# A fused cross-attention kernel: another order of VectorE's and GpSimd's instructions within a step

## The chip, the cores and the metric

One core of one Trainium2 chip runs the whole kernel. The metric is the device time in microseconds (us) of one execution. An engine here is TensorE (PE in the profile, its weight loads PEld), VectorE (DVE), ScalarE (ACT), GpSimd (POOL) or SyncE (SP), which issues the transfers. Each engine works through its own list of instructions in order, and waits at semaphores for the others and, where it reads what it has just written, for itself.

## The reference

With x of shape (4, 2048, 512) and ctx of shape (4, 77, 384), all float32:

```python
text_p = x @ W_text + b_text                       # 512 -> 512
audio_p = ctx @ W_audio + b_audio                  # 384 -> 512
Q = layer_norm(text_p, g1, beta1)
K = layer_norm(audio_p, g2, beta2)
alpha = softmax(Q @ K.T / sqrt(512))               # 77 keys
out = layer_norm((alpha @ audio_p) @ W_out + b_out + x, g_out, beta_out)
```

The layer norms divide by the root of the variance over 512 features plus 1e-5. All three need a row statistic that is ready only after a product.

## The kernel before, in words

The prologue (about 55 us) folds the small matrices together: the scores of a row of x are one product with a matrix `proj` of its batch (77 score columns, a mean column and the 512 columns of a quadratic form whose dot product with x is the variance of the projected row), and values times `W_out` are one matrix per batch. What is left runs in 32 steps of 256 rows. A step takes the rows as two halves, t = 0 and t = 1, of 128 rows each; below `x_lo`(0) is `x_lo` of the first half. Steps go over the four batches in turn. The engines work at several steps at once: `lag` in the code is how many steps behind the newest one an instruction works.

For a half, in order of the data:

- SP loads 128 rows of x into `xs`, as soon as `hid` of the same half four steps back has been made.
- TensorE transposes them into the one bank `psT` (L1253). ScalarE copies that to `x_hi` (L619), VectorE makes the rest `x_lo` (L854). TensorE's next transposes wait for that `x_lo`, since they write `psT` again.
- TensorE multiplies `x_hi` and `x_lo` with `proj` into two banks (L1322, L1326, then L1333). VectorE adds a constant to the first bank's scores, `sc_part` (L946), adds the second bank's to that, `xs<-psY,sc_part` (L954; the scores lie beside the rows of x), and takes the quadratic sum (L956).
- Once per step VectorE clamps the statistics, `stat_eps` (L968); GpSimd raises them to the power -1/2, `rstd` (L470), and makes `shift2` from it (L474; its tile is `shift` in the rows).
- VectorE makes the `logits` of both halves (L985), then their maximum `neg_max` (L988). ScalarE takes the exponentials into `psD` (L670) and rounds them into `parts` (L678); VectorE makes the rest of `parts` (L997, L998) and `inv_sum`, the reciprocal of the sums (L993).
- TensorE transposes `parts` into `psE` (L1303, L1304), between L1326 and L1333 of the second half; ScalarE copies that to `parts_t` (L684); TensorE multiplies it with the values into the one bank `psO` (L1345).
- VectorE makes `hid` from `psO`, `inv_sum` and `xs` (L976). ScalarE squares it for the variance (L650) and normalises it into `zs` (L661). GpSimd multiplies `zs` by `gain` (L458) and adds `shift` (L464). SP stores a step's 256 rows when both halves' sums are made (L354).

What sets the order of every engine is written out by hand: one function `body` per engine with calls in a fixed order, repeated for each step, and a tail for the last two steps in which calls are written one by one. ScalarE's order in a step is `x_hi`(0), square(0), normalise(0), exponentials, rounding, `x_hi`(1), `parts_t`, square(1), normalise(1). TensorE's is transposes(0), values product(0), `proj` product(0), values product(1), transposes(1), `proj` product(1) with the turned `parts` in between. In the tail GpSimd makes the powers one by one (L487); VectorE's `last_logits` (L1081) wait for them.

Of the kernel before, what the change touches and what calls it, by code (L numbers as in the profile page):

```python
# [33 lines left out]
def cross_attention(nc, x, ctx, w_text, b_text, w_audio, b_audio, w_out, b_out,  # L34
                    g1, beta1, g2, beta2, g_out, beta_out, out):
    B, L, D = x.shape
# [27 lines left out]
    with ExitStack() as stack:  # L64
# [183 lines left out]
        LAST = STEPS - 1  # L248
# [137 lines left out]
        def _(pool):  # L386
# [67 lines left out]
            def gain_of(b, i, t, lag):  # L454

                q = (b - lag) % B
                wait_if_positive(pool, z_ready, T, i, T * (b - lag) + t + 1)
                nc.gpsimd.tensor_tensor(zs[:, q, t, :], zs[:, q, t, :], gain[:], ALU.mult).then_inc(zg_ready, 1)  # L458

            def shift_of(b, i, t, lag):  # L460

                q = (b - lag) % B
                wait_if_positive(pool, zg_ready, T, i, T * (b - lag) + t + 1)
                nc.gpsimd.tensor_tensor(zs[:, q, t, :], zs[:, q, t, :], shift[:], ALU.add).then_inc(out_ready, 1)  # L464

            def body(b, i, live):

                if live(2) or live(4):
                    wait_if_positive(pool, stat_ready, 1, i, b - 1)
                    nc.gpsimd.tensor_tensor(rstd[:, b, :], stat_eps[:, b, :], neg_half[:], ALU.pow).then_inc(rstd_ready, 1)  # L470
                if live(4):
                    q = (b - 4) % B
                    wait_if_positive(pool, rstd_ready, 1, i, b - 1)
                    nc.gpsimd.tensor_tensor(shift2[:, q, :], sc[:, q, :, NX], rstd[:, b, T:2 * T], ALU.mult).then_inc(shift2_ready, 1)  # L474
                if live(5):
                    gain_of(b, i, 1, 5)
                    shift_of(b, i, 1, 5)
                if live(4):
                    gain_of(b, i, 0, 4)
                    shift_of(b, i, 0, 4)  # L480

            written_out(body)


# [4 lines left out]
            def mean_shift(n, j):  # L489
                pool.wait_ge(rstd_ready, n)  # L490
                nc.gpsimd.tensor_tensor(shift2[:, j % B, :], sc[:, j % B, :, NX], rstd[:, j % B, T:2 * T], ALU.mult).then_inc(shift2_ready, 1)

            def late_gain(j, t):
                pool.wait_ge(z_ready, T * j + t + 1)
                nc.gpsimd.tensor_tensor(zs[:, j % B, t, :], zs[:, j % B, t, :], gain[:], ALU.mult).then_inc(zg_ready, 1)

            def late_shift(j, t):
                pool.wait_ge(zg_ready, T * j + t + 1)
                nc.gpsimd.tensor_tensor(zs[:, j % B, t, :], zs[:, j % B, t, :], shift[:], ALU.add).then_inc(out_ready, 1)

            inverse_root(STEPS - 1, (LAST + 1) % B, 0, 2 * T)
            mean_shift(STEPS - 1, LAST - 3)
            late_gain(LAST - 4, 1)
            late_shift(LAST - 4, 1)
            inverse_root(STEPS, (LAST + 2) % B, 0, 1)
            late_gain(LAST - 3, 0)
# [264 lines left out]
        def _(dve):  # L771
# [207 lines left out]
            def shifted_logits(b, i):  # L979
                q = (b - 2) % B  # L980
                wait_if_positive(dve, rstd_ready, 1, i, b - 1)
                wait_if_positive(dve, sc_ready, T, i, T * (b - 2) + T)
                wait_if_positive(dve, prob_ready, T, i, T * (b - 4) + T)
                for t in range(T):
                    nc.vector.scalar_tensor_tensor(logits[:, b % 2, t, :], sc[:, q, t, 1:1 + S], rstd[:, b, t:t + 1],  # L985
                                                   score_d[:, q, :], ALU.mult, ALU.add).then_inc(logits_ready, 1)
                wait_if_positive(dve, logits_ready, T, i, T * (b - 2) + T)
                nc.vector.reduce_max(neg_max[:, q, :], logits[:, b % 2, :, :], axis=AX_X, negate=True).then_inc(max_ready, 1)  # L988

# [11 lines left out]
            def body(b, i, live):  # L1001
                if live(2):
                    scores_and_quad(b - 1, i, 1)
                if live(2) or live(4):
                    guard(b, i, live)
                if live(3):
                    residual(b, i, 0)
                if live(0):
                    lo_part(b, i, 0)
                if live(2):  # L1010
                    shifted_logits(b, i)
                if live(1):
                    part_of_scores(b, i, 0)
                    scores_and_quad(b, i, 0)
                if live(2):
                    prob_rest(b, i)
                if live(3):
                    residual(b, i, 1)
                if live(0):
                    lo_part(b, i, 1)  # L1020
                if live(2):
                    inverse_sum(b, i)
                if live(1):
                    part_of_scores(b, i, 1)


            written_out(body)
# [2 lines left out]
            END = STEPS // B  # L1030
# [63 lines left out]
            residual(0, END, 0)  # L1094
            shifted_logits(0, END)
            part_of_scores(0, END, 0)
            scores_and_quad(0, END, 0)
            prob_rest(0, END)
            score_guard(0, 1, T * LAST + 1)
# [332 lines left out]
```

## Time and profile before

| what | value |
|---|---|
| median of 3 runs | 271.93 us (271.63 to 275.46) |
| profiled execution | 271.35 us, its span 269.6 us |
| TensorE's granted clock, mean of the span | 0.993 |
| TensorE busy | 257.3 us (95%) |
| VectorE busy | 238.0 us (88%) |
| ScalarE busy | 202.1 us (75%) |
| GpSimd busy | 209.3 us (78%) |

Busy time counts the stretches in which an instruction ran, overlaps once. The span is the profiled stretch from the first to the last instruction; the execution's own time has 1.75 us more around it. A start-to-start distance between two neighbours on one engine says more than their durations, since an instruction may begin before the one ahead of it has ended.

### The profile page before, as it was taken

To read this page: it belongs to the slowest core of one execution; us is meant where nothing else is said; L and a number is where in the kernel's file an instruction comes from. 1 tells how busy PE (TensorE), PEld (TensorE's weight loads), DVE (VectorE), ACT (ScalarE), POOL (GpSimd) and SP (SyncE) were. 2 spreads that over 40 slices of the span, in tenths; PEclk is the share of its full clock that TensorE was granted. 3 is DMA by queue.
4 is the path that set the end of the run, shared out by engine and by line. 5 is a ranking of instruction groups with operands and counts; after the bars stand their busy time and mean duration, and the time that the engine had idled before them with its cause. 6 is when DMAs were issued, how large, how long until landed. Compare 5 with 4: busy or idle time off the path is not lost.

```text
span 269.6 us, 5946 instructions
## 1 busy us (share of the span) xinstructions
PE 257.3 (95%) x1667; PEld 232.3 (86%) x1667; DVE 238.0 (88%) x719; ACT 202.1 (75%) x516; POOL 209.3 (78%) x232
## 2 busy tenths in 40 slices
PE   7899999999999999999999999999999999999970
PEld 6678868899999999999999999989999999999830
DVE  3858479879999999999999999899999999999894
ACT  3775267246788888888888888888888888888981
POOL 6075630011599999999999999999999999999985
PEclk9999999999999999999999999999999999999997
DMA  6905199332225445444454444544444444444217
GB/s 203 317 30 186 42 340 347 108 126 91 79 77 189 163 175 172 165 160 163 158 163 169 168 163 153 161 156 156 157 157 157 156 156 156 156 158 168 94 49 272
DMA packets 19456, 43.25 MB, mean 160 GB/s; under 512 B 2050, under 2 KB 2382, under 8 KB 19434
## 3 DMA queue, kind: packets, MB, share of 16 engines
q1 hardware_dynamic: 18810, 41.96, 46.0%
q10 hardware_dynamic: 624, 1.06, 1.2%
q14 instruction: 16, 0.13, 0.2%
q8 instruction: 6, 0.10, 0.1%
HBM read 21.19 MB, written 16.78 MB: 141 GB/s over the span
## 4 chain that ended last, share of the span: by engine, by line
DVE 63%; PE 14%; issue 10%; POOL 5%; ACT 2%; DMA 2%; SPq 1%; DVEq 0%; POOLq 0%; ACTq 0%
DVE x_lo L854 13%; DVE hid L976 13%; DVE waste_dve L956 12%; DVE xs L954 5%; DVE logits L985 5%; DVE neg_max L988 3%; DVE sc_part L946 3%; DMA zs<-in_ctx_dram 2%; DVE parts L998 2%; PE psY L1145 2%; PE psT L1220 1%; DVE stat L956 1%; PE psY L1220 1%; PE psT L1170 1%; POOL zs L464 1%
## 5 line engine op out<-in xcount | busy, mean ns | idle before, releaser
L1322 PE MATMUL psY<-proj,x_hi 128*128 128x336 f32 x512 | 92.4, 322 | 0.0
L1322 PEld LDWEIGHTS psY<-proj,x_hi 128*128 128x128 f32 x512 | 80.8, 188 | 2.8
L464 POOL TENSOR_TENSOR zs<-zs,shift 128x512 f32<-128x512 f32 x55 | 71.0, 1291 | 4.3
L458 POOL TENSOR_TENSOR zs<-zs,gain 128x512 f32<-128x512 f32 x55 | 70.9, 1289 | 1.0 <-ACT zs L661 1.0
L470 POOL TENSOR_TENSOR rstd<-stat_eps,neg_half 128x4 f32<-128x4 f32 x30 | 30.5, 1017 | 32.2 <-DVE stat_eps L968 32.2
L1333 PE MATMUL psY<-proj,x_lo 128*128 128x336 f32 (+1 forms) x256 | 50.5, 319 | 0.0
L956 DVE CUSTOM_DVE_ANT_0 waste_dve<-psY,xs,sums 128x515 bf16<-128x515 f32 x64 | 48.4, 757 | 2.2
L650 ACT ACTIVATE waste_act<-hid,xs 128x512 bf16<-128x512 f32 x60 | 43.0, 717 | 8.6 <-DVE hid L976 8.6
L661 ACT ACTIVATE zs<-hid,shift,rstd 128x512 f32<-128x512 f32 x59 | 47.5, 805 | 0.0
L976 DVE SCALAR_TENSOR_TENSOR hid<-psO,inv_sum,xs 128x512 f32<-128x512 f32 x60 | 44.8, 746 | 0.1
L854 DVE TENSOR_TENSOR x_lo<-psT,x_hi 128x512 fp32r<-128x512 f32 x64 | 43.5, 680 | 0.7 <-ACT x_hi L619 0.5
L619 ACT ACTIVATE x_hi<-psT 128x512 fp32r<-128x512 f32 x64 | 37.6, 588 | 5.7 <-PE psT L1253 5.7
L1253 PE MATMUL psT<-ident,xs 128*128 128x128 f32 x256 | 40.1, 279 | 0.4
L1333 PEld LDWEIGHTS psY<-proj,x_lo 128*128 128x128 f32 x256 | 39.0, 189 | 0.0
L1253 PEld LDWEIGHTS psT<-ident,xs 128*128 128x128 f32 x256 | 29.5, 140 | 10.6 <-DVE x_lo L854 5.0
L684 ACT ACTIVATE parts_t<-psE 128x512 fp32r<-128x512 f32 x31 | 18.6, 599 | 22.5 <-PE psE L1304 22.5
L1345 PE MATMUL psO<-wo_hi,parts_t 128*128 128x512 f32 x60 | 26.7, 445 | 0.1
L1345 PE MATMUL psO<-wo_lo,parts_t 103*128 103x512 f32 x60 | 23.7, 394 | 0.0
L1326 PEld LDWEIGHTS psY<-proj,x_lo 128*128 128x128 f32 x128 | 22.1, 188 | 0.0
L954 DVE TENSOR_TENSOR xs<-psY,sc_part 128x79 f32<-128x79 f32 x64 | 15.4, 240 | 7.5 <-PE psY L1333 0.7
L1326 PE MATMUL psY<-proj,x_lo 128*128 128x256 f32 (+1 forms) x128 | 21.7, 251 | 0.0
L670 ACT ACTIVATE psD<-logits,neg_max 128x77 f32<-128x77 f32 x62 | 19.1, 309 | 2.3 <-DVE neg_max L988 2.3
(264 smaller groups left out, 418.3 us busy)
## 6 DMA issues: line engine op xcount, KB each, us to landing
xs<-in_x_dram SPq DMA_DIRECT2D x64, 256.0 KB, 3.0
out_dram<-zs SPq DMA_DIRECT2D x29, 512.0 KB, 3.9
proj<-proj SPq DMA_DIRECT2D x4, 768.0 KB, 8.5
out_dram<-zs SPq DMA_DIRECT2D x6, 256.0 KB, 2.1
xs<-in_L_xattn_W_text_dram SPq DMA_DIRECT2D x4, 256.0 KB, 3.6
xs<-in_L_xattn_W_out_dram SPq DMA_DIRECT2D x2, 512.0 KB, 4.3
wa<-in_L_xattn_W_audio_dram SPq DMA_DIRECT2D x1, 768.0 KB, 6.3
zs<-in_ctx_dram SPq DMA_DIRECT2D x1, 462.0 KB
```

What stands on the lines that cost most here:

```text
L458: nc.gpsimd.tensor_tensor(zs[:, q, t, :], zs[:, q, t, :], gain[:], ALU.mult).then_inc(zg_ready, 1)
L464: nc.gpsimd.tensor_tensor(zs[:, q, t, :], zs[:, q, t, :], shift[:], ALU.add).then_inc(out_ready, 1)
L650: nc.scalar.activation(waste_act[:, t, :], hid[:, (b - 3) % 2, t, :], ACT.Square, bias=sc[:, q, t, NX:NX + 1], accum_out=stat[:, (b + 1) % ...
L661: nc.scalar.activation(zs[:, q, t, :], hid[:, b % 2, t, :], ACT.Identity, bias=shift2[:, q, t:t + 1], scale=rstd[:, b, T + t:T + t + 1]).t ...
L854: nc.vector.tensor_tensor(x_lo[:, b % 2, t, :], psT[:], f32(x_hi[:, b % 2, t, :]), ALU.subtract).then_inc(x_lo_ready, 1)
L956: nc.vector.tensor_tensor_reduce(out=waste_dve[:, t, 0:QUAD_W], in0=psY[:, t, QUAD_AT:QUAD_AT + QUAD_W], in1=xs_rows[:, q, t, X_AT - 1:X_A ...
L976: nc.vector.scalar_tensor_tensor(hid[:, (b - 3) % 2, t, :], psO[:], inv_sum[:, q, t:t + 1], xs[:, q, t, :], ALU.mult, ALU.add).then_inc(hi ...
L1253: last = nc.tensor.transpose(psT[:, k * P:(k + 1) * P], xs[:, b, t, k * P:(k + 1) * P], ident[:])
L1322: nc.tensor.matmul(psY[:, t, to:to + HALF], x_hi[:, par, t, k * P:(k + 1) * P], proj[:, q, k, right * HALF:(right + 1) * HALF], start=(k = ...
L1326: last = nc.tensor.matmul(psY[:, t, B_AT + SW + k * P:512], x_lo[:, par, t, k * P:(k + 1) * P], proj[:, q, k, SW + k * P:HALF], start=Fals ...
L1333: last = nc.tensor.matmul(psY[:, t, 512 + skip:512 + HALF], x_lo[:, par, t, k * P:(k + 1) * P], proj[:, q, k, HALF + skip:ROW_W], start=Fa ...
L1345: last = nc.tensor.matmul(psO[:], parts_t[0:rows, (b - lag) % 2, t, n, :], v[0:rows, q, :], start=(n == 0), stop=(n == 1))
```

## The change

TensorE's, ScalarE's and SP's lists stay as they are. VectorE's `sc_part` of the second half moves from behind the reciprocal to in front of `x_lo` of the second half; the maximum becomes a call of its own, `largest`, and stands behind `sc_part` of the first half; the reciprocal moves ahead of the rest of `parts`. GpSimd makes both products and then both sums of one step, all five steps behind, where it had made the second half five behind and the first half four behind, each product followed by its sum. The tails of both engines are adapted.

```diff
                 if live(5):
+                    gain_of(b, i, 0, 5)
                     gain_of(b, i, 1, 5)
+                    shift_of(b, i, 0, 5)
                     shift_of(b, i, 1, 5)
-                if live(4):
-                    gain_of(b, i, 0, 4)
-                    shift_of(b, i, 0, 4)
...
             mean_shift(STEPS - 1, LAST - 3)
+            late_gain(LAST - 4, 0)
             late_gain(LAST - 4, 1)
+            late_shift(LAST - 4, 0)
             late_shift(LAST - 4, 1)
             inverse_root(STEPS, (LAST + 2) % B, 0, 1)
...
+            def largest(b, i):
+                q = (b - 2) % B
                 wait_if_positive(dve, logits_ready, T, i, T * (b - 2) + T)
                 nc.vector.reduce_max(neg_max[:, q, :], logits[:, b % 2, :, :], axis=AX_X, negate=True).then_inc(max_ready, 1)
...
                 if live(1):
                     part_of_scores(b, i, 0)
+                if live(2):
+                    largest(b, i)
+                if live(1):
                     scores_and_quad(b, i, 0)
                 if live(2):
+                    inverse_sum(b, i)
                     prob_rest(b, i)
                 if live(3):
                     residual(b, i, 1)
+                if live(1):
+                    part_of_scores(b, i, 1)
                 if live(0):
                     lo_part(b, i, 1)
-                if live(2):
-                    inverse_sum(b, i)
-                if live(1):
-                    part_of_scores(b, i, 1)
...
             part_of_scores(0, END, 0)
+            largest(0, END)
             scores_and_quad(0, END, 0)
```

VectorE's list in a full step before, from `logits` to the second `sc_part` (L946 is `sc_part`, L854 `x_lo`, L956 the quadratic sum and the read of its accumulator):

```order
L985 SCALAR_TENSOR_TENSOR logits<-xs,rstd,psD 128x77 x2
L988 TENSOR_REDUCE neg_max<-logits 128x2
L946 TENSOR_TENSOR sc_part<-psY,score_c 128x79
L954 TENSOR_TENSOR xs<-psY,sc_part 128x79
L956 ISA waste_dve,stat<-psY,xs,sums 128x515
L956 ISA stat 128x1
L997 TENSOR_TENSOR parts<-psD,parts 128x2x51
L998 TENSOR_TENSOR parts<-psD,parts 128x2x26
L976 SCALAR_TENSOR_TENSOR hid<-psO,inv_sum,xs 128x512
L854 TENSOR_TENSOR x_lo<-psT,x_hi 128x512
L993 RECIPROCAL inv_sum<-prob_sum 128x2
L946 TENSOR_TENSOR sc_part<-psY,score_c 128x79
```

The same piece of the changed kernel, whose line numbers are one to four higher:

```order
L986 SCALAR_TENSOR_TENSOR logits<-xs,rstd,psD 128x77 x2
L947 TENSOR_TENSOR sc_part<-psY,score_c 128x79
L992 TENSOR_REDUCE neg_max<-logits 128x2
L955 TENSOR_TENSOR xs<-psY,sc_part 128x79
L957 ISA waste_dve,stat<-psY,xs,sums 128x515
L957 ISA stat 128x1
L997 RECIPROCAL inv_sum<-prob_sum 128x2
L1001 TENSOR_TENSOR parts<-psD,parts 128x2x51
L1002 TENSOR_TENSOR parts<-psD,parts 128x2x26
L977 SCALAR_TENSOR_TENSOR hid<-psO,inv_sum,xs 128x512
L947 TENSOR_TENSOR sc_part<-psY,score_c 128x79
L855 TENSOR_TENSOR x_lo<-psT,x_hi 128x512
```

Each `sc_part` now has another instruction between itself and its reader `xs`, and the second one stands between `hid` and `x_lo`.

GpSimd's list at the end before, from the last full body's last product to the power for `last_logits(0)` (`128x1`) and the one after it:

```order
L458 TENSOR_TENSOR zs<-zs,gain 128x512
L464 TENSOR_TENSOR zs<-zs,shift 128x512
L487 TENSOR_TENSOR rstd<-stat_eps,neg_half 128x4
L491 TENSOR_TENSOR shift<-xs,rstd 128x2
L495 TENSOR_TENSOR zs<-zs,gain 128x512
L499 TENSOR_TENSOR zs<-zs,shift 128x512
L487 TENSOR_TENSOR rstd<-stat_eps,neg_half 128x1
L495 TENSOR_TENSOR zs<-zs,gain 128x512
L487 TENSOR_TENSOR rstd<-stat_eps,neg_half 128x3
```

And in the changed kernel:

```order
L458 TENSOR_TENSOR zs<-zs,gain 128x512 x2
L464 TENSOR_TENSOR zs<-zs,shift 128x512 x2
L486 TENSOR_TENSOR rstd<-stat_eps,neg_half 128x4
L490 TENSOR_TENSOR shift<-xs,rstd 128x2
L494 TENSOR_TENSOR zs<-zs,gain 128x512 x2
L498 TENSOR_TENSOR zs<-zs,shift 128x512 x2
L486 TENSOR_TENSOR rstd<-stat_eps,neg_half 128x1
L494 TENSOR_TENSOR zs<-zs,gain 128x512
L486 TENSOR_TENSOR rstd<-stat_eps,neg_half 128x3
```

Between the four-column power and the one-column power there are now four instructions on 128x512 where there were two.

## Rows read from the trace of the kernel before

**Rows 1.** The page: busy time by engine, and the chain that ended last.
```profile
PE 257.3 (95%) x1667; PEld 232.3 (86%) x1667; DVE 238.0 (88%) x719; ACT 202.1 (75%) x516; POOL 209.3 (78%) x232
...
DVE 63%; PE 14%; issue 10%; POOL 5%; ACT 2%; DMA 2%; SPq 1%; DVEq 0%; POOLq 0%; ACTq 0%
```

**Rows 2.** Timeline, VectorE, one steady step: start us, duration us, engine, line, operation.
```profile
162.15 0.26 DVE L997 TENSOR_TENSOR parts<-psD,parts 128x102 fp32r<-128x102 f32 x1
...
162.45 0.74 DVE L976 SCALAR_TENSOR_TENSOR hid<-psO,inv_sum,xs 128x512 f32<-128x512 f32 x1
163.11 0.68 DVE L854 TENSOR_TENSOR x_lo<-psT,x_hi 128x512 fp32r<-128x512 f32 x1
163.71 0.16 DVE L993 RECIPROCAL inv_sum<-prob_sum 128x2 f32<-128x2 f32 x1
163.78 0.22 DVE L946 TENSOR_TENSOR sc_part<-psY,score_c 128x79 f32<-128x79 f32 x1
164.11 0.24 DVE L954 TENSOR_TENSOR xs<-psY,sc_part 128x79 f32<-128x79 f32 x1
...
165.29 0.75 DVE L976 SCALAR_TENSOR_TENSOR hid<-psO,inv_sum,xs 128x512 f32<-128x512 f32 x1
165.96 0.68 DVE L854 TENSOR_TENSOR x_lo<-psT,x_hi 128x512 fp32r<-128x512 f32 x1
166.56 0.49 DVE L985 SCALAR_TENSOR_TENSOR logits<-xs,rstd,psD 128x77 f32<-128x77 f32 x2
167.08 0.31 DVE L988 TENSOR_REDUCE neg_max<-logits 128x2 f32<-128x154 f32 x1
...
168.65 0.26 DVE L997 TENSOR_TENSOR parts<-psD,parts 128x102 fp32r<-128x102 f32 x1
```

**Rows 3.** Timeline, ScalarE, the same stretch; in brackets idle time and its releaser.
```profile
161.01 0.31 ACT L670 ACTIVATE psD<-logits,neg_max 128x77 f32<-128x77 f32 x1
...
161.82 0.30 ACT L678 ACTIVATE parts<-psD 128x154 fp32r<-128x154 f32 x1
...
166.08 0.72 ACT L650 ACTIVATE waste_act<-hid,xs 128x512 bf16<-128x512 f32 x1 [0.25 <-DVE hid L976]
...
171.73 0.58 ACT L619 ACTIVATE x_hi<-psT 128x512 fp32r<-128x512 f32 x1
```

**Rows 4.** Timeline, TensorE: a `proj` product of the second half, the next transposes.
```profile
162.50 0.34 PE L1326 MATMUL psY<-proj,x_lo 128*128 128x256 f32 x2
...
163.85 0.42 PEld L1253 LDWEIGHTS psT<-ident,xs 128*128 128x128 f32 x4 [0.21 <-DVE x_lo L854]
```

**Rows 5.** Timeline, GpSimd, the same step.
```profile
165.42 1.02 POOL L470 TENSOR_TENSOR rstd<-stat_eps,neg_half 128x4 f32<-128x4 f32 x1
...
166.66 1.29 POOL L458 TENSOR_TENSOR zs<-zs,gain 128x512 f32<-128x512 f32 x1
168.03 1.30 POOL L464 TENSOR_TENSOR zs<-zs,shift 128x512 f32<-128x512 f32 x1
...
169.27 1.30 POOL L458 TENSOR_TENSOR zs<-zs,gain 128x512 f32<-128x512 f32 x1
```

**Rows 6.** Timeline, GpSimd and VectorE, the tail.
```profile
251.53 1.30 POOL L495 TENSOR_TENSOR zs<-zs,gain 128x512 f32<-128x512 f32 x1
...
252.91 1.27 POOL L499 TENSOR_TENSOR zs<-zs,shift 128x512 f32<-128x512 f32 x1
...
254.13 0.56 POOL L487 TENSOR_TENSOR rstd<-stat_eps,neg_half 128x1 f32<-128x1 f32 x1
...
254.72 0.29 DVE L1081 SCALAR_TENSOR_TENSOR logits<-xs,rstd,psD 128x77 f32<-128x77 f32 x1
```

**Rows 7.** Chain of work that ended last: start us, share in us, what; the tail.
```profile
254.17 0.53 POOL rstd L487
```

**Rows 8.** Timeline, SP's queue, one output store; and the page on the loads of x.
```profile
170.47 0.35 SPq L354 DMA_DIRECT2D out_dram<-zs  x1
...
xs<-in_x_dram SPq DMA_DIRECT2D x64, 256.0 KB, 3.0
```

## The prediction

> **What bounds the kernel now.** I read the page first [rows 1]: TensorE is busy 95% of the span, VectorE 88%, GpSimd 78%, and the chain that ended last lies 63% on VectorE. So a balanced pipeline, with VectorE ahead on the path; what matters is the period of one step. Then one steady step in order of time. VectorE's rows [rows 2] repeat after 168.65 - 162.15 = 6.50 us and show no idle time. But the two ends of the step are not alike: the 128x512 instructions start 0.07 to 0.08 us before the end of the one in front (0.74 us of `hid`, next start after 0.66), while an instruction that needs the result just written starts late: `xs` 0.33 us after an `sc_part` of 0.22, `neg_max` 0.52 after `logits` of 0.49.
>
> ScalarE's rows [rows 3] show that VectorE is not alone. The `hid` at 165.29 in [rows 2] is the first half's; its end at 166.04 releases the square at 166.08, and from there ScalarE runs to the rounding that ends at 162.12 (one step earlier), after which `parts` starts at 162.15. So the circle that sets the period is: `hid`(0) at 165.29, through ScalarE, to `parts` at 168.65 (3.36 us), then VectorE's own rows to the next `hid`(0): 165.29 - 162.15 = 3.14. Sum 6.50.
>
> TensorE [rows 4] waits once per step: its first transposes at 163.85 come 0.06 after the end of `x_lo`(1) (163.11 + 0.68 = 163.79), 0.21 of it idle. Without that it would need 6.50 - 0.21 = 6.29.
>
> GpSimd [rows 5]: a sum starts 1.37 after its product, an independent one 1.24. A step is 165.42 to 166.66 (1.24), then 1.37 + 1.24 + 1.37 + about 1.25 = 6.47. So it has 0.03 to spare, and an edit on VectorE alone would stop there.
>
> **The change, part by part.** (0) and (1) are the halves of a step.
>
> VectorE. Nothing is added or removed; 3 of its rows move. (a) The second `sc_part` goes in front of `x_lo`(1), so its successor `xs` no longer waits for it: 0.33 becomes the 0.22 less 0.07, 0.15; saves 0.18. (b) The first `sc_part` goes between `logits` and `neg_max`: again 0.18 at its successor, and at `neg_max` 0.52 becomes 0.49 - 0.07 = 0.42; saves 0.10. (c) The reciprocal moves ahead of `parts`; it keeps its 0.07 (163.71 to 163.78). VectorE's own work falls from about 6.45 to about 6.0, and the circle above from 6.50 to 3.36 + 3.14 - 0.18 - 0.07 = 6.25; (b) gains nothing in it, because that stretch is covered by ScalarE.
>
> GpSimd. Both sums have a product of the other half between: two times 1.37 - 1.25 = 0.12, so 6.47 becomes 6.23. Worth nothing by itself, while other circles are longer.
>
> So far it looks like 6.29, TensorE's own rate, a gain of 0.2 per step. What is late next decides. TensorE's wait for `x_lo`(1) is on a longer circle of two steps, and the change puts two `sc_part` into exactly this one. From [rows 2 to 4]:
> - transposes at 163.85 to ScalarE's `x_hi`(0) at 171.73: 7.88 (through TensorE's turned probabilities, `parts_t`, second square, second normalisation, all in ScalarE's order)
> - `x_hi` 0.58 and 0.03 to VectorE (as 162.12 to 162.15): 0.61
> - `x_lo`(0) to `logits`: 0.60
> - `logits` to `neg_max`: 0.52 before; after, 0.42 + 0.15 = 0.57
> - `neg_max` 0.31 and 0.04 to ScalarE (as 166.04 to 166.08): 0.35
> - exponentials and rounding, 161.01 to 162.12: 1.11, and 0.03 to `parts`
> - `parts` to `hid`(1): 0.30; `hid`(1) to the next: 0.66
> - new here: `sc_part`(1), 0.15
> - `x_lo`(1) 0.68 and 0.06 to the transposes: 0.74
>
> Before: 12.80 for two steps, 6.40 each, hidden under 6.50. After: 13.00, **6.50 each**. The gaps are taken out where VectorE has room and 0.20 goes in where TensorE waits. I take +0.0 to +0.02 per step; over the 28 steps or so in which every stage is live (32 in all, in halves the 64 `x_lo`) **+0.3 us**. Its bounds: 0.1 either way on the circle of 13.00 (twelve joints of 0.01) is 0.05 per step, 1.4 us.
>
> The end. A step's first-half product and sum used to be made four bodies behind it, now five, like the second half's. At the end two of them (LAST - 4, half 0) stand ahead of the power that `last_logits(0)` needs. Before, product 251.53, sum 252.91, power 254.13, which is 2.60 after the product; VectorE's `logits` at 254.72 starts 0.03 after that power's end (254.13 + 0.56) [rows 6]. After: product, product, sum, sum, power = 4 x 1.25 = 5.00. So it comes 5.00 - 2.60 = **2.4 us** later, VectorE's queue stands behind its wait, and TensorE's last transposes and ScalarE's last exponentials behind that. The chain of waits goes through this power, 254.17 in [rows 7], and on through `logits` to the last instruction, each step released by the one before, so I charge all of it. At the start the two that are not made early save nothing: GpSimd sat idle there.
>
> The output store. It waits for a step's last sum, formerly the second of GpSimd's four, now the fourth: some 2.5 us later, less what the queue waited anyway [rows 8]: it was issued at 170.47, the sum it needs was done at 168.03 + 1.30 = 169.33, and now would be at about 171.7. Next on SP's queue is the load of `x`, which waits for `hid`(0) at about 172.5 and is not held; it has 166.04 + 3.0 (its median to landing) = 169.04 against the transposes at 170.34 as a pattern [rows 4], 1.3 to spare for its greater overlap with the store. Cost 0; if all 1.3 were used up, a loss that begins there.
>
> Sum: 271.35 (the profiled execution, span 269.6 and 1.75 around it; median of the runs 271.93, 0.6 above) + 0.3 + 2.4 = 274.05, said as **274.0 us**, 0.8% over the median.
>
> **Rivals.**
> *TensorE's own rate is reached.* Everything for it but the circle of 13.00; if two or three joints are covered, the period falls to 6.29, -0.21 x 28 = -5.9, with the end's 2.4: 267.9. Chance 0.09, and only with the end free as well (265.5) faster by 2%: 0.03 of these.
> *The end costs nothing*, if something late in the tail swallows it: 271.6. The unbroken chain speaks against it. Chance 0.08.
> *Slower: `sc_part` delays whatever comes after it.* Every row of `sc_part` is followed by `xs`, so none shows that the 0.33 comes from the result and not from `sc_part` itself. If it is its own, the two that moved into the circle cost 0.33 each rather than 0.15: 13.36, 6.68 per step, +0.18 x 28 = +5.0, with the end 278.8. It decides (277.4 is 2% over) from 277.4 - 271.35 - 2.4 = 3.65, 0.13 per step, that is a spacing of 0.28. Against it: `hid`, `x_lo` and `neg_max` all let an independent one start early. Chance 0.06.
> The Trainium skill (VectorE: DVE Perf Modes, The DRAIN you can't avoid) says that eight chained copies take the same time with a semaphore after each as with one at the end, so that the semaphore costs nothing. By that rule the 0.33 would stay and the sum would be 278.8, by the rows 274.0; the early starts of independent instructions in [rows 2] disagree with it.
> *Slower: the second `sc_part` now holds `x_lo`(1) for TensorE.* It needs the product whose records end at 162.84, 5.48 after that step's transposes (163.85 less 6.49); it is due at 6.50 - 0.06 - 0.68 - 0.15 = 5.61. With 0.04 for the joint that is 0.09 to spare; only if the end is really 0.22 later does the step pass 6.63, and the sum 277.4. Chance 0.04.
> The Trainium skill (Perfetto Trace Analysis, Tensor Engine Instruction) says that a matmul's end in the trace is modelled; no run here shows how far off this one is.
>
> **Numbers.** Forecast 0.73, the rivals 0.09, 0.08, 0.06, 0.04. The forecast's own range is 274.0 with 1.4 each way and the end between 1.4 and 2.4; taking in the free end below and part of the slower cases above gives 270.2 (the free end, 1.4 lower) to 276.8. Two per cent, 5.4 us, is about what runs that spread from 271.63 to 275.46 can tell: faster 0.03, within 0.87, slower 0.10.
>
> **What would show it.** Right: the gap in front of `xs` gone (0.15 or a wait for TensorE), the idle time of TensorE's first transposes grown to 0.25 or more rather than gone, `x_hi` appearing as a releaser of `x_lo`(0), perhaps steps of 6.4 and 6.6 in turn, GpSimd idle 0.2 to 0.3 per step before its power, and the power of `last_logits(0)` 2.4 later behind its predecessor. Wrong: TensorE without a wait at a period of 6.3; or `x_lo`(1) starting 0.33 after `sc_part`; or `logits` in the tail waiting for something other than GpSimd.

## The result, and the profile after

| | before | changed |
|---|---|---|
| median, 20 runs each | 272.22 us (270.91 to 276.01) | 274.82 us (273.5 to 277.36) |
| profiled execution, span | 271.35, 269.6 | 273.82, 272.1 |
| first four-column power to the last one (30 steps) | 55.51 to 250.29: 194.78 | 55.16 to 250.38: 195.22 |
| start of that last power to start of GpSimd's last sum | 15.21 | 17.60 |

The ratio of the changed kernel to the one before is **1.0101** (95% interval 1.0077 to 1.0126); the forecast of 274.0 us lies 0.3% under the measured median. The last two lines of the table are two stretches of the profiled execution: the steps took 0.44 more, the end 2.39 more. The forecast had 0.3 and 2.4. (The profiled execution as a whole took 2.47 more, since its first power came 0.35 earlier.) Ratios and intervals, here and below, leave out executions over 1.5% slower than the fastest of the same kernel.

The chain that ended last, from the changed kernel's page, against [rows 1]:

```profile
PE 49%; DVE 23%; ACT 12%; issue 8%; POOL 4%; DMA 2%; ACTq 1%; POOLq 0%; DVEq 0%; SPq 0%
```

VectorE's share of the chain fell from 63% to 23%, and TensorE's rose from 14% to 49%; the time did not follow. The bound moved, it didn't get shorter.

VectorE's timeline, changed kernel, one step; start, duration, engine, line, operation, idle time in brackets:

```profile
160.57 0.49 DVE L986 SCALAR_TENSOR_TENSOR logits<-xs,rstd,psD 128x77 f32<-128x77 f32 x2
160.98 0.23 DVE L947 TENSOR_TENSOR sc_part<-psY,score_c 128x79 f32<-128x79 f32 x1
161.13 0.30 DVE L992 TENSOR_REDUCE neg_max<-logits 128x2 f32<-128x154 f32 x1
161.35 0.23 DVE L955 TENSOR_TENSOR xs<-psY,sc_part 128x79 f32<-128x79 f32 x1
...
162.29 0.17 DVE L997 RECIPROCAL inv_sum<-prob_sum 128x2 f32<-128x2 f32 x1
162.63 0.26 DVE L1001 TENSOR_TENSOR parts<-psD,parts 128x102 fp32r<-128x102 f32 x1 [0.17 <-ACT parts L679]
...
162.93 0.74 DVE L977 SCALAR_TENSOR_TENSOR hid<-psO,inv_sum,xs 128x512 f32<-128x512 f32 x1
163.59 0.23 DVE L947 TENSOR_TENSOR sc_part<-psY,score_c 128x79 f32<-128x79 f32 x1
163.73 0.68 DVE L855 TENSOR_TENSOR x_lo<-psT,x_hi 128x512 fp32r<-128x512 f32 x1
164.42 0.24 DVE L955 TENSOR_TENSOR xs<-psY,sc_part 128x79 f32<-128x79 f32 x1
```

The gaps of [rows 2] are gone: 0.15 and 0.14 from an `sc_part` to the next start, where it was 0.33; `logits` to `neg_max` is 0.41 + 0.15 = 0.56, forecast 0.57. What VectorE saved comes back in part as a wait for ScalarE, 0.17 per step in front of `parts`.

The weight loads of TensorE's transposes in two steps, changed kernel, against [rows 4]: the first half's, the second half's, and so on.

```profile
164.47 0.42 PEld L1260 LDWEIGHTS psT<-ident,xs 128*128 128x128 f32 x4 [0.30 <-DVE x_lo L855]
167.70 0.59 PEld L1260 LDWEIGHTS psT<-ident,xs 128*128 128x128 f32 x4
170.88 0.42 PEld L1260 LDWEIGHTS psT<-ident,xs 128*128 128x128 f32 x4
...
177.51 0.42 PEld L1260 LDWEIGHTS psT<-ident,xs 128*128 128x128 f32 x4 [0.35 <-DVE x_lo L855]
```

The long wait for `x_lo`(1) is now in every second step: 164.47 to 170.88 is 6.41, 170.88 to 177.51 is 6.63. The other steps wait too, only shorter: the timeline prints no idle time under 0.15, but the load queue was done at 170.13 + 0.61 = 170.74, and 170.88 is 0.05 after the end of that step's `x_lo`(1) (170.15 + 0.68). So the waits are 0.14 and 0.30 in turn, 0.22 on average, where the kernel before had 0.21 in each step. GpSimd's four-column power alternates with it, against [rows 5]:

```profile
159.31 1.02 POOL L470 TENSOR_TENSOR rstd<-stat_eps,neg_half 128x4 f32<-128x4 f32 x1 [0.30 <-DVE stat_eps L969]
165.73 1.02 POOL L470 TENSOR_TENSOR rstd<-stat_eps,neg_half 128x4 f32<-128x4 f32 x1
172.31 1.02 POOL L470 TENSOR_TENSOR rstd<-stat_eps,neg_half 128x4 f32<-128x4 f32 x1 [0.30 <-DVE stat_eps L969]
```

Steps of 6.42 and 6.58, 6.50 on average. The rows along the prediction's two-step circle, ScalarE's and VectorE's, from `x_hi`(0) to the transposes at 170.88:

```profile
165.77 0.58 ACT L620 ACTIVATE x_hi<-psT 128x512 fp32r<-128x512 f32 x1
166.38 0.69 DVE L855 TENSOR_TENSOR x_lo<-psT,x_hi 128x512 fp32r<-128x512 f32 x1
166.99 0.49 DVE L986 SCALAR_TENSOR_TENSOR logits<-xs,rstd,psD 128x77 f32<-128x77 f32 x2
167.55 0.30 DVE L992 TENSOR_REDUCE neg_max<-logits 128x2 f32<-128x154 f32 x1
167.89 0.33 ACT L671 ACTIVATE psD<-logits,neg_max 128x77 f32<-128x77 f32 x1
...
168.71 0.30 ACT L679 ACTIVATE parts<-psD 128x154 fp32r<-128x154 f32 x1
...
169.05 0.27 DVE L1001 TENSOR_TENSOR parts<-psD,parts 128x102 fp32r<-128x102 f32 x1 [0.16 <-ACT parts L679]
...
169.35 0.74 DVE L977 SCALAR_TENSOR_TENSOR hid<-psO,inv_sum,xs 128x512 f32<-128x512 f32 x1
170.00 0.23 DVE L947 TENSOR_TENSOR sc_part<-psY,score_c 128x79 f32<-128x79 f32 x1
170.15 0.68 DVE L855 TENSOR_TENSOR x_lo<-psT,x_hi 128x512 fp32r<-128x512 f32 x1
```

With the first transposes of two steps earlier at 157.88 the joints are 7.89, 0.61, 0.61, 0.56, 0.34, 1.16 (to `parts`), 0.30, 0.65, 0.15 and 0.73, in sum 13.00; none is more than 0.02 off the prediction's.

The profile's own chain mostly takes another way, which the prediction didn't price. From 158.00 to 164.47, for one, it goes from the second half's `xs`, released by TensorE's product (L1340), through the quadratic sum, `hid`(0), ScalarE's square(0) and normalisation(0), the exponentials, `parts`, `hid`(1) and `sc_part`(1) to the transposes, and from there through TensorE's products of one step to the next `xs`(1). This circle is also one of two steps and has `sc_part`(1) in it once, but not `parts_t`, the second square and the second normalisation. By the rows it is 0.07 shorter. A normalisation starts at 160.69 and the next ScalarE instruction could start 0.71 later (as in number 10 below), at 161.40; the exponentials start at 161.47, 0.04 after `neg_max` has ended (161.13 + 0.30). So the prediction's circle ends last, by 0.07 in 13.00, and number 10 below tests which of the two it is.

The tail of the changed kernel, GpSimd and then VectorE's wait, against [rows 6]:

```profile
251.62 2.53 POOL L494 TENSOR_TENSOR zs<-zs,gain 128x512 f32<-128x512 f32 x2
254.10 2.54 POOL L498 TENSOR_TENSOR zs<-zs,shift 128x512 f32<-128x512 f32 x2
256.60 0.56 POOL L486 TENSOR_TENSOR rstd<-stat_eps,neg_half 128x1 f32<-128x1 f32 x1
...
257.19 0.29 DVE L1087 SCALAR_TENSOR_TENSOR logits<-xs,rstd,psD 128x77 f32<-128x77 f32 x1 [2.48 <-POOL rstd L486]
```

The power comes at 256.60, 2.47 later than in [rows 6, 7], and VectorE stands idle for 2.48 of it.

### The profile page after: what moved, and what is told of

It reads as the page before. It is cut to its first block, busy times and chain, and to the rows that moved or that the text cites. A ratio compares the mean times of both kernels' runs of the same rounds, so it can differ in the third digit from the quotient of the medians.

```text
span 272.1 us, 5946 instructions
## 1 busy us (share of the span) xinstructions
PE 256.5 (94%) x1667; PEld 232.1 (85%) x1667; DVE 236.7 (87%) x719; ACT 203.9 (75%) x516; POOL 207.6 (76%) x232
## 4 chain that ended last, share of the span: by engine, by line
PE 49%; DVE 23%; ACT 12%; issue 8%; POOL 4%; DMA 2%; ACTq 1%; POOLq 0%; DVEq 0%; SPq 0%
PE psY L1329 15%; PE psY L1340 7%; DVE hid L977 7%; PE psT L1260 6%; PE psO L1352 5%; ACT zs L662 3%; DVE x_lo L855 3%; DVE waste_dve L957 3%; ACT psD L671 3%; PE psY L1333 2%; DMA xs<-in_x_dram 2%; PE psY L1152 2%; DVE xs L955 2%; ACT parts L679 1%; PE psE L1310 1%
## 5 line engine op out<-in xcount | busy, mean ns | idle before, releaser
L458 POOL TENSOR_TENSOR zs<-zs,gain 128x512 f32<-128x512 f32 x54 | 68.7, 1293 | 0.0
L464 POOL TENSOR_TENSOR zs<-zs,shift 128x512 f32<-128x512 f32 x54 | 68.5, 1292 | 0.0
L1340 PE MATMUL psY<-proj,x_lo 128*128 128x336 f32 (+1 forms) x256 | 50.5, 319 | 0.0
L1340 PEld LDWEIGHTS psY<-proj,x_lo 128*128 128x128 f32 x256 | 39.0, 189 | 0.0
L671 ACT ACTIVATE psD<-logits,neg_max 128x77 f32<-128x77 f32 x62 | 19.7, 317 | 2.4 <-DVE neg_max L992 2.4
```

The costliest lines, as they stand in the source:

```text
L1340: last = nc.tensor.matmul(psY[:, t, 512 + skip:512 + HALF], x_lo[:, par, t, k * P:(k + 1) * P], proj[:, q, k, HALF + skip:ROW_W], start=Fa ...
```

## The experiments

All ratios are to runs of the kernel before that were taken beside them on the same chip, with 95% intervals. "Steps" and "end" are the two stretches of the table above, read in one profiled execution of each kernel.

| kernel | ratio | steps | end |
|---|---|---|---|
| before | 1 | 194.78 | 15.21 |
| changed | 1.0101 (1.0077 to 1.0126) | 195.22 | 17.60 |
| 1 VectorE's list alone | 1.0006 (0.9956 to 1.0057) | 194.79 | 15.23 |
| 2 GpSimd's list alone | 1.0128 (1.0072 to 1.0185) | 194.95 | 17.65 |
| 3 changed, first half four behind | 0.9999 (0.9963 to 1.0035) | 195.35 | 15.24 |
| 4 changed, `x_lo`(1) ahead of `sc_part`(1) | 1.0026 (0.9977 to 1.0075) | 193.05 | 17.59 |
| 5 before, two swapped, GpSimd in pairs | 0.9949 (0.9915 to 0.9984) | 194.16 | 15.23 |
| 6 changes of 3 and 4 together | 0.9908 (0.9877 to 0.9940) | 192.88 | 15.24 |
| 7 before, two swapped | 0.9959 (0.9918 to 1.0001) | 194.06 | 15.23 |
| 8 changed, `sc_part`(1) twice | 1.0185 (1.0141 to 1.0228) | 197.23 | 18.31 |
| 9 changed, power earlier in the tail | 1.0062 (1.0015 to 1.0108) | 194.84 | 16.87 |
| 10 changed, normalisation moved | 1.0058 (1.0009 to 1.0107) | 194.24 | 18.38 |

**1 to 4: which half of the change costs what.** Number 1 has GpSimd's functions of the kernel before:

```diff
                 if live(5):
-                    gain_of(b, i, 0, 5)
                     gain_of(b, i, 1, 5)
-                    shift_of(b, i, 0, 5)
                     shift_of(b, i, 1, 5)
+                if live(4):
+                    gain_of(b, i, 0, 4)
+                    shift_of(b, i, 0, 4)
```

(and its tail). 

> VectorE's list of the changed kernel, GpSimd's of the kernel before. Circle and end (the forecast's theory): the two-step circle of 13.00 still holds, 6.50 to 6.52 per step with steps of 6.4 and 6.6 in turn, and with the second half's product and sum alone in front of the one-column power nothing is lost at the end: 271.7, ratio to before 1.001. TensorE's rate was within reach and only the end took it back: 6.3 per step, 266 to 268, ratio 0.98. The loss lies in VectorE's steps and not in the end: 274.4, ratio 1.010. Between: should GpSimd's own list, 6.45 to 6.47, matter, its idle time before the power is 0.

Number 2 is the same edit the other way round, made to the kernel before. 

> VectorE's list of the kernel before, GpSimd's of the changed one (both halves five steps behind, product, product, sum, sum, also in the tail). Circle and end: the one-step circle of 3.36 + 3.14 stays at 6.50 per step, GpSimd gets 0.2 to 0.3 of idle time per step before its four-column power and gives nothing back, and the one-column power for the last logits comes 2.4 later: 273.8, ratio 1.009. Rival, the end is covered: ratio 1.000. Rival, GpSimd's step of 6.47 was the bound and the pairing frees it: 6.43 per step, -2 and +2.4, ratio 1.001.

Number 3 keeps the pairs, without the fifth step:

```diff
                 if live(5):
-                    gain_of(b, i, 0, 5)
                     gain_of(b, i, 1, 5)
-                    shift_of(b, i, 0, 5)
+                if live(4):
+                    gain_of(b, i, 0, 4)
+                if live(5):
                     shift_of(b, i, 1, 5)
+                if live(4):
+                    shift_of(b, i, 0, 4)
```

(with the tail of before.) 

> The changed kernel with GpSimd's two products and two sums still in pairs, but of the second half five steps behind and of the first half four behind, and the tail of the kernel before: it differs from the changed kernel only in how far behind the first half is made. Circle and end: the steps stay at 6.50 to 6.52, the end comes 2.4 earlier than in the changed kernel: 271.7, ratio to before 1.001. Rival, the lag costs nothing and the steps do: 274.4, ratio 1.010. Rival, the first half's product right behind its own power waits for the normalised rows and stalls GpSimd: over 6.6 per step, ratio over 1.012.

Number 4 is the changed kernel with two calls in VectorE's body exchanged:

```diff
-                if live(1):
-                    part_of_scores(b, i, 1)
                 if live(0):
                     lo_part(b, i, 1)
+                if live(1):
+                    part_of_scores(b, i, 1)
```

> The changed kernel with one swap: in each step x_lo of the second half stands ahead of sc_part of the second half, as before the change. Two-step circle: its 0.15 for sc_part goes out, 13.00 becomes 12.85, and since xs then waits for sc_part again (0.33 in place of 0.15) the one-step circle is 6.25 + 0.18 = 6.43; 6.43 to 6.44 per step, -0.07 x 28 = -2.0 against the changed kernel's 273.8: 271.9, ratio to before 1.001 (the end's 2.4 stays). Rival, TensorE's or GpSimd's rate and not this circle: no change from the changed kernel, ratio 1.010. Rival, the gap behind sc_part costs VectorE the same wherever it lies: a step of 6.50 or more, ratio 1.009 to 1.012.

In the changed kernel and numbers 1 to 7 the column "end" has two levels: 15.2 wherever the first half is four steps behind, 17.6 wherever it is five behind. VectorE's list doesn't touch it. So the loss of the changed kernel comes with GpSimd's lag, shown from both sides (2 has it without VectorE's edit, 1 and 3 don't have it with VectorE's edit). In the steps, neither half of the change gains anything. Number 2 came out above its expected 1.009, which its interval holds: its profile has 0.17 more in the steps and 2.44 more at the end.

In number 1 one detail failed: for a dozen steps no 6.4 and 6.6 in turn but even steps of 6.50, GpSimd without a printed idle time and 61% of the chain on it. The steps of its profile are at full clock (granted clock 1.00 from 20 to 255 us; it was 0.53 and 0.79 from 10 to 15 and 15 to 20 us). A circle of two steps fixes only the sum of two, 13.00, and even steps of 6.50 fit it as well as uneven ones; number 9, with the changed kernel's body, goes over from 6.42 and 6.58 to 6.50 and 6.50 in its last steps. Number 7 returns to GpSimd.

Number 4 agrees with the circle. Its steps are even and shorter; GpSimd's four-column powers:

```profile
158.43 1.02 POOL L470 TENSOR_TENSOR rstd<-stat_eps,neg_half 128x4 f32<-128x4 f32 x1 [0.18 <-DVE stat_eps L969]
...
164.87 1.02 POOL L470 TENSOR_TENSOR rstd<-stat_eps,neg_half 128x4 f32<-128x4 f32 x1 [0.17 <-DVE stat_eps L969]
```

6.44, as expected, though VectorE does the same instructions and now stalls again between `sc_part` and `xs`:

```profile
162.62 0.68 DVE L855 TENSOR_TENSOR x_lo<-psT,x_hi 128x512 fp32r<-128x512 f32 x1
163.22 0.23 DVE L947 TENSOR_TENSOR sc_part<-psY,score_c 128x79 f32<-128x79 f32 x1
163.55 0.24 DVE L955 TENSOR_TENSOR xs<-psY,sc_part 128x79 f32<-128x79 f32 x1
```

The start of `xs` is 0.33 after `sc_part` here: one of the dependent pairs that the change removes is back, and the kernel is 2.2 us shorter in its steps than with the change. Of these, 28 steps of 0.06 are 1.7; some 0.45 is a late load of x that only the changed kernel's profile has (step of 6.97, below). The gap was worth less than the place in front of `x_lo`(1).

**5 to 7: what is left to gain.** Number 5 is made from the kernel before, with GpSimd's pairs of number 3 and this in VectorE's body:

```diff
-                if live(2):
-                    inverse_sum(b, i)
                 if live(1):
                     part_of_scores(b, i, 1)
+                if live(2):
+                    inverse_sum(b, i)
```

> From the kernel before, two edits. VectorE: the reciprocal and sc_part of the second half change places (hid, x_lo, sc_part, reciprocal, xs), so that the reciprocal lies in the gap in front of xs. GpSimd: in pairs, first half four steps behind, tail as before. Circles: the one-step circle loses the 0.07 of the reciprocal, 6.50 to 6.43; the two-step circle stays at 12.80 (6.40); GpSimd 6.23. So 6.43 per step with GpSimd idle 0.15 to 0.2 before its power, -0.07 x 28 = -2.0 from 271.35: 269.4, ratio to before 0.993. Rival, TensorE's rate and not a circle sets the step: 6.29, ratio 0.978. Rival, the reciprocal in the gap makes xs wait again for itself: 6.50, ratio 1.000.

Number 6 is number 3 with number 4's exchange. 

> The changed kernel's VectorE list with x_lo of the second half ahead of sc_part of the second half, and GpSimd in pairs with the first half four steps behind and the tail of the kernel before: the two parts that cost something are taken out of the change. 6.44 per step as in the previous run with that swap, and no loss at the end: 271.35 - 0.06 x 28 = 269.7, ratio to before 0.994. Rival, the loss at the end does not depend on how far behind the first half is: 272, ratio 1.003.

Number 7 is number 5 without the pairs. 

> Only VectorE's swap of the reciprocal and sc_part, GpSimd as before. In the first run GpSimd's list of before ran at exactly 6.50 with no idle time in 13 steps, so it is a bound of its own beside VectorE's circle of 6.50: then the swap alone gives nothing, 6.50, ratio to before 1.000, GpSimd without idle time and the chain of waits on it. Rival, GpSimd's list takes 6.45 to 6.47 as added up in the prediction, and VectorE's circle was the only one at 6.50: 6.45 to 6.47, ratio 0.995.

Number 7's VectorE and GpSimd:

```profile
163.85 0.23 DVE L946 TENSOR_TENSOR sc_part<-psY,score_c 128x79 f32<-128x79 f32 x1
164.00 0.15 DVE L993 RECIPROCAL inv_sum<-prob_sum 128x2 f32<-128x2 f32 x1
164.19 0.24 DVE L954 TENSOR_TENSOR xs<-psY,sc_part 128x79 f32<-128x79 f32 x1
```

```profile
159.11 1.02 POOL L470 TENSOR_TENSOR rstd<-stat_eps,neg_half 128x4 f32<-128x4 f32 x1
...
160.35 1.29 POOL L458 TENSOR_TENSOR zs<-zs,gain 128x512 f32<-128x512 f32 x1
161.72 1.29 POOL L464 TENSOR_TENSOR zs<-zs,shift 128x512 f32<-128x512 f32 x1
162.97 1.29 POOL L458 TENSOR_TENSOR zs<-zs,gain 128x512 f32<-128x512 f32 x1
...
165.59 1.01 POOL L470 TENSOR_TENSOR rstd<-stat_eps,neg_half 128x4 f32<-128x4 f32 x1
```

The reciprocal fits into the gap (`sc_part` to `xs` 0.34, with 0.19 of it after the reciprocal's start), and GpSimd has no idle time at a step of 6.48. In the steps from 94.36 to 230.48 it averages 6.48. My expectation of 6.50 fell, its rival of 6.45 to 6.47 was nearer: I had read number 1's 6.50 as GpSimd's own, and the prediction's sum of 6.47 for GpSimd was right to 0.01. The conclusion stays: GpSimd's list, at 0.02 under the circle, stops whoever shortens VectorE's circle alone. With the pairs (number 5) GpSimd has room again, idle 0.16 to 0.17 in front of its power, and most steps take 6.43 to 6.44. The rest of its 194.16 is in a few long steps; the longest (7.23) follows a wait of 0.85 that TensorE has at 99.23 for a late load of x. Numbers 5 and 6 beat both kernels, 6 by 0.9% (0.6 to 1.2); between 5 and 6 the intervals overlap. Number 6 is the change without its two mistakes: what is left of VectorE's reordering, and GpSimd's pairs, gain only without `sc_part`(1) in front of `x_lo`(1) and without the fifth step of lag. That the pairs are needed for it is argued from GpSimd's 6.48 in number 7; number 6's VectorE list was not run without them.

**8: the circle, loaded.** The same `sc_part` again, into a tile that nobody reads:

```diff
+                if t == 1:
+                    nc.vector.tensor_tensor(extra[:], psY[:, t, B_AT:B_AT + SC], score_c[:, q, :], ALU.add)
                 nc.vector.tensor_tensor(sc_part[:, t, :], psY[:, t, B_AT:B_AT + SC], score_c[:, q, :], ALU.add).then_inc(part_ready, 1)
```

> The changed kernel with the second half's sc_part made twice, first into a tile that nobody reads (0.15 more between hid and x_lo of the second half, no added wait). Two-step circle: 13.00 + 0.15 = 13.15, so 6.57 per step, half of the added 0.15, +0.075 x 28 = +2.1 over the changed kernel: 275.9, ratio to before 1.018. Rival, a circle of one step through VectorE holds the changed kernel: all of the 0.15 counts, 6.65, +4.2, ratio 1.026. Rival, TensorE's or GpSimd's own rate: nothing, ratio 1.010.

Its VectorE:

```profile
160.35 0.74 DVE L980 SCALAR_TENSOR_TENSOR hid<-psO,inv_sum,xs 128x512 f32<-128x512 f32 x1
161.01 0.24 DVE L949 TENSOR_TENSOR extra<-psY,score_c 128x79 f32<-128x79 f32 x1
161.17 0.23 DVE L950 TENSOR_TENSOR sc_part<-psY,score_c 128x79 f32<-128x79 f32 x1
161.32 0.68 DVE L856 TENSOR_TENSOR x_lo<-psT,x_hi 128x512 fp32r<-128x512 f32 x1
```

and the powers of GpSimd:

```profile
156.74 1.02 POOL L471 TENSOR_TENSOR rstd<-stat_eps,neg_half 128x4 f32<-128x4 f32 x1 [0.31 <-DVE stat_eps L972]
...
163.34 1.02 POOL L471 TENSOR_TENSOR rstd<-stat_eps,neg_half 128x4 f32<-128x4 f32 x1 [0.34 <-DVE stat_eps L972]
...
169.91 1.02 POOL L471 TENSOR_TENSOR rstd<-stat_eps,neg_half 128x4 f32<-128x4 f32 x1 [0.32 <-DVE stat_eps L972]
```

0.16 more per step on VectorE, and 13.17 for two steps where it was 13.00: half of it per step, as a circle of two steps gives. A circle of one step would have given all of it. In all the steps it is 2.0, and 2.45 without the changed kernel's late load, against 28 x 0.085 = 2.4. This doesn't tell the two circles of two steps apart: both have `sc_part`(1) once.

The end grew by 0.7 as well, which nobody forecast. 0.16 of it is the second `sc_part`, made once in the tail too: TensorE's last transposes come 10.24 after the last four-column power, 10.08 in the changed kernel. The rest goes with the granted clock. In the 8 us from 263.63 it was 0.57 here, in the same stretch of the changed kernel (from 258.38) 1.00, and a values product (L1390 there, L1393 here) that took 0.51 us took 0.99. TensorE stood idle for 3.0 us in front of its last transposes in the changed kernel as well; why the clock fell in one profile and not in the other isn't shown.

**9: the end.** The second half's product and sum of step LAST - 4 move behind the one-column power:

```diff
             late_gain(LAST - 4, 0)
-            late_gain(LAST - 4, 1)
             late_shift(LAST - 4, 0)
-            late_shift(LAST - 4, 1)
             inverse_root(STEPS, (LAST + 2) % B, 0, 1)
+            late_gain(LAST - 4, 1)
+            late_shift(LAST - 4, 1)
             late_gain(LAST - 3, 0)
```

> The changed kernel with another order in GpSimd's tail alone: of step LAST - 4 the first half's product and sum stand ahead of the one-column power, the second half's behind it, so that again one product and one sum stand in front of it as before the change; the work is the same. The end's theory (what counts is how late the powers for the last logits come): the one-column power comes 2.4 earlier than in the changed kernel, but the three-column power behind it then has three 128x512 instructions in front of it in place of one; from the rows of the changed kernel, 254.2 + 0.56 + 1.38 + 1.25 + 1.25 = 258.6, which is 0.7 earlier than its 259.31. So the end comes 0.7 to 0.9 earlier: 273.0, ratio to before 1.007. Rival, the end goes by how much work GpSimd has left in all: no change, ratio 1.010. Rival, the one-column power alone matters: 2.4 earlier, 271.4, ratio 1.001. The steps stay at 6.50 on average.

Its tail, on GpSimd:

```profile
254.69 0.56 POOL L486 TENSOR_TENSOR rstd<-stat_eps,neg_half 128x1 f32<-128x1 f32 x1
...
259.04 0.86 POOL L486 TENSOR_TENSOR rstd<-stat_eps,neg_half 128x3 f32<-128x3 f32 x1
```

and on VectorE:

```profile
255.29 0.30 DVE L1087 SCALAR_TENSOR_TENSOR logits<-xs,rstd,psD 128x77 f32<-128x77 f32 x1
...
259.93 0.29 DVE L1087 SCALAR_TENSOR_TENSOR logits<-xs,rstd,psD 128x77 f32<-128x77 f32 x1 [1.13 <-POOL rstd L486]
```

The wait moved from the first `logits` to the second, and the end is 0.73 shorter than in the changed kernel with the same work, as much as the three-column power comes earlier (8.20 after the last four-column power, where it was 8.93): what counts is when the powers come.

**10: the circle's leg through ScalarE.**

```diff
+                if live(4):
+                    normalise(b, i, 1)
                 if live(2):
                     parts_out(b, i)
                 if live(3):
                     square(b, i, 1)
-                if live(4):
-                    normalise(b, i, 1)
```

> The changed kernel with one edit on ScalarE: the second half's normalisation stands ahead of parts_t, where ScalarE waits 0.78 to 0.94 for TensorE, and no longer behind the second square. It takes 0.71 out of the leg of the two-step circle that runs through ScalarE (parts_t, second square, second normalisation, x_hi) and leaves VectorE's and GpSimd's lists alone. Two-step circle: TensorE's wait for x_lo of the second half shrinks and the steps stop alternating, the next circle takes over at 6.45 to 6.48: -0.03 to -0.04 x 28, about -1.0 against the changed kernel, 272.8, ratio to before 1.006. Rival, the circle has no leg through ScalarE's normalisation: nothing changes, ratio 1.010, the steps still alternate. Rival, normalising early holds parts_t up: slower, over 6.55 per step, ratio over 1.016.

ScalarE in this kernel, and TensorE's first transposes in two steps one after the other:

```profile
163.07 0.82 ACT L662 ACTIVATE zs<-hid,shift,rstd 128x512 f32<-128x512 f32 x1
164.08 0.60 ACT L685 ACTIVATE parts_t<-psE 128x512 fp32r<-128x512 f32 x1 [0.19 <-PE psE L1311]
```

```profile
158.10 0.42 PEld L1260 LDWEIGHTS psT<-ident,xs 128*128 128x128 f32 x4 [0.17 <-DVE x_lo L855]
...
164.57 0.42 PEld L1260 LDWEIGHTS psT<-ident,xs 128*128 128x128 f32 x4 [0.19 <-DVE x_lo L855]
```

The waits of 0.14 and 0.30 in turn have become 0.17 to 0.19 in each, the steps take 6.44 to 6.48 from 134 to 211 us, and the whole stretch is 1.0 shorter: an edit on another engine that touches the same circle gains what was expected, with VectorE's and GpSimd's lists as they were. This run tells the two circles of two steps apart. It takes 0.71 out of the prediction's circle and nothing out of the other, and 13.00 became 12.92, which is the other's 12.93. So the prediction's circle held the changed kernel, with the other 0.07 behind it.

Here too the end grew, by 0.8. TensorE's last transposes still come 10.08 after the last four-column power, as in the changed kernel; what follows is longer, at a granted clock of 0.58 in the 8 us from 257.93, against 1.00 in the changed kernel's, with a values product of 0.99 us in place of 0.51. So this is the clock of the profiled execution, as in number 8, and not the early normalisation.

## Why the prediction was right

- **VectorE's gaps.** 0.33 to 0.15 at `xs`, 0.52 to 0.42 at `neg_max`: measured 0.15, 0.14 and 0.41. Right. The rival by which `sc_part` delays whatever comes after it is out: `x_lo`(1) starts 0.14 after it, and number 7's reciprocal 0.15. By the rule of the Trainium skill that the prediction weighed (VectorE: DVE Perf Modes, The DRAIN you can't avoid: eight chained copies take as long with a semaphore after each as with one at the end), read as the prediction read it, the 0.33 would have stayed; the rows of the changed kernel disagree with 0.15. The same section also says that a next instruction that is not held starts earlier, and with that they agree.
- **The circle of one step at 6.25.** It is no longer the bound; VectorE waits 0.17 per step for ScalarE instead. No run shows the 6.25 itself. That this circle was the bound before, at 6.50, is shown by number 2, where GpSimd's list has 0.21 to 0.22 to spare and the steps stay at 6.49 to 6.50, and by number 5, where taking 0.07 out of it gives 6.43; in number 7 GpSimd's 6.48 comes first.
- **The circle of two steps, 12.80 to 13.00.** This is what the answer hung on. Shown by its joints in the rows, 13.00, and by three kernels that each change one of them: `sc_part`(1) taken out 12.88 (number 4; this circle would be 12.85 and the one-step circle 6.43 per step, which the run can't tell apart), doubled 13.17 (number 8), and 0.71 taken out on ScalarE 12.92 (number 10, where the circle through `xs`(1) takes over, which the prediction didn't have). That this circle was in front of that one by only 0.07, and not behind it, was luck: the prediction never priced the other.
- **The steps, +0.3.** They came to +0.44, and that this is so near is in part chance. The changed kernel's profile has a load of x for which TensorE waited 0.48 at 99.47, in a step of 6.97; the profile of the kernel before has two long steps (6.80 and 6.66) worth 0.46 that the changed kernel has not. The rest is 0.2 in the first seven steps and under 0.01 per step after them: two regular steps took 12.99 before and 13.00 after. The forecast of 0.0 to 0.02 per step was right.
- **The signs.** The idle time of TensorE's first transposes grew only in every second step (0.30; 0.14 in the others), on average hardly (0.21 to 0.22). It had to be so at the same 6.50 per step; the sign "0.25 or more" asked too much. GpSimd's idle time before its power is likewise 0.30 in every second step. `x_hi` does release `x_lo`(0): 166.38 is 0.03 after 165.77 + 0.58.
- **GpSimd's pairs worth nothing by themselves.** Number 2's steps are 0.17 longer in all than before, not shorter, with 0.21 to 0.22 of idle time in front of its power. Right. But "0.03 to spare" was the whole distance to the next bound, and by the steps it decides between numbers 5 and 7 of the experiments (6.43 against 6.48; their ratios overlap).
- **The end, 2.4.** Measured 2.39, at a granted clock of 1.00 up to the last transposes in both profiles. Right, and number 9 shows the mechanism, not only the size.
- **The store order at no cost.** The changed kernel's store was issued at 172.20 and the next load at 173.12; the loads' median to landing went from 3.0 to 2.9, the stores' fell from 3.9 to 2.8, against [rows 8]. No steady cost. One late load is in the profiles of the changed kernel and of numbers 3, 5 and 10 (0.5 to 0.9 of TensorE's time) and of numbers 2 and 9 (0.2), all with GpSimd in pairs, and in none of the three without pairs (before, 1 and 7); but it is missing in three others with pairs (4, 6 and 8). Whether the pairs, and with them the later store, cause it is open; if they do, the term that the prediction put at nothing is some 0.5.
- **TensorE's own rate, 6.29.** Not reached in any of the twelve kernels. The best average is 6.43, and the changed kernel's short steps of 6.41 still have 0.14 of waiting in TensorE's load queue.

## What to carry to other kernels

Before taking a gap out of an engine's list, ask which wait of the other engines the filler now stands in front of. Here an `sc_part` of 0.15, put in front of the `x_lo` for which TensorE waits, cost more than closing the gap of 0.18 gave (net some 1.7 us over the steps, number 4 against the change). Look for circles that close only after two steps: they can show as steps of two lengths in turn (in number 9 they became even), and a delay in one costs half per step. Such a circle can have a neighbour a few hundredths behind it, and then a cut in one leg gains only down to the neighbour (number 10: 0.71 taken out, 0.08 gained). And price the end of a pipeline apart from its steps: one more step of lag on an engine that is not the bottleneck cost 2.4 us here, more than any reordering of the steps gained (1.9, number 6).

## What was not expected of the hardware

- The profiled executions differ mostly ahead of the steps, and the difference goes with the granted clock. The first four-column power came between 55.02 and 59.82 us in the twelve profiles, while the 30 steps of the changed kernel and of number 9, which have the same order there, take 195.22 and 194.84. In the eight profiles in which it came by 56.01 the granted clock was 1.00 from 10 to 15 us; in the four in which it came at 57.61, 58.40, 58.48 and 59.82 (numbers 6, 8, 3 and 1) it was 0.66, 0.71, 0.68 and 0.53. In the tail the same cost numbers 8 and 10 some 0.6 and 0.8 us. A kernel should be compared by its steps and its end, with the clock of each stretch beside them, and its medians only over many runs.
- GpSimd too starts later behind a result of its own. In number 7 a sum starts 1.37 after the product that it reads (160.35 to 161.72), the next product, which reads nothing from that sum, 1.25 after it (161.72 to 162.97), at a duration of 1.29. VectorE and GpSimd thus show the same pattern here, a start that comes before the end of the instruction in front when nothing is read from it.
